# Column sums of the adjacency matrix moved from the first phase to the sweep of the next layer, and row sums by pairwise additions

## The reference

```
# layer 0
adj_hat = adj + eye(n);  d = 1 / sqrt(adj_hat.sum(axis=1))       # row sums
x = x + (d[:,None] * adj_hat * d[None,:]) @ h @ W.T + b
# layer 1: same normalisation, relu
x = x + relu((d[:,None] * adj_hat * d[None,:]) @ (h @ weight))
# layer 2 (attention): uses, besides learned attention matrices,
Rf = S / clip(S.sum(axis=1), 1e-12)                              # row sums again
Rb = S / clip(S.sum(axis=0), 1e-12)[:,None]                      # column sums, S = adj + eye(n)
# layer 3
x = x + (1-t) * (h @ weight) + t * (adj @ (h @ weight))
```

## Time and profile before

| | us |
|---|---|
| median of 3 runs (lowest to highest) | 3489.06 (3486.54 to 3490.57) |
| time of the profiled execution | 3488.64 |
| span of its records | 3486.8 |
| mean granted TensorE clock, share of 2.4 GHz | 0.957 |
| busy in the span: PE, PEld, DVE, ACT, POOL | 3144.3, 2272.6, 2454.0, 1599.1, 2146.4 |

### The profile page before, as it was taken

One profiled execution on the slowest core, in us unless ns is written; L12 is line 12 of the kernel. 1 busy time (PEld: TensorE's weight loads), 2 busy tenths in 40 slices (PEclk: granted clock), 3 DMA queues, 4 the chain that ended last, 5 costly groups with the idle time before them and its releaser, 6 DMA issues. The chain is left out here.

```text
span 3486.8 us, 42119 instructions
## 1 busy us (share of the span) xinstructions
PE 3144.3 (90%) x13212; PEld 2272.6 (65%) x13212; DVE 2454.0 (70%) x3451; ACT 1599.1 (46%) x2357; POOL 2146.4 (62%) x4214
## 2 busy tenths in 40 slices
PE   4999989998699999999976698988899999996899
PEld 3788878885477777777754254544566566664788
DVE  6983410002998889888884799999978999998000
ACT  2211321225566666666653455555555655552200
POOL 1212421124788888888880677877988788886211
PEclk9999999998899999999988899999999999998899
DMA  6643444443122122112211111211222222223254
GB/s 246 223 162 132 130 147 163 163 142 86 44 58 58 58 58 66 54 59 63 65 33 62 47 52 52 62 44 56 57 81 76 73 84 82 74 83 102 91 201 172
DMA packets 140702, 327.59 MB, mean 94 GB/s; under 512 B 15456, under 2 KB 93664, under 8 KB 129248
## 3 DMA queue, kind: packets, MB, share of 16 engines
q1 hardware_dynamic: 140512, 325.30, 29.3%
HBM read 286.70 MB, written 38.54 MB: 93 GB/s over the span
## 5 line engine op out<-in xcount | busy, mean ns | idle before, releaser
L1027 ACT ACTIVATE junk<-E,negp 128x3327 uint8<-128x3327 f32 x208 | 637.3, 3064 | 142.4 <-issue 107.8
L1399 DVE SCALAR_TENSOR_TENSOR U<-E,trial 128x3327 f32<-128x3327 f32 x182 | 678.5, 3728 | 0.0
L922 PE MATMUL bank<-big,adj 128*128 128x512 f32 x1352 | 609.9, 602 | 8.7 <-ACT t L1053 8.7
L922 PEld LDWEIGHTS bank<-big,adj 128*128 128x128 f32 x1352 | 252.9, 192 | 329.2 <-issue 328.1
L294 PE MATMUL bank<-big,E 128*128 128x256 f32 x1664 | 366.2, 381 | 2.4 <-PEq L58 1.7
L882 PE MATMUL bank<-Hc,PT 128*128 128x256 f32 x1248 | 305.1, 396 | 69.2 <-ACT PT L1066 69.2
L294 PEld LDWEIGHTS bank<-big,E 128*128 128x128 f32 x1664 | 315.9, 191 | 49.3 <-issue 6.6
L882 PE MATMUL bank<-Hc,adj 128*128 128x256 f32 x1456 | 335.4, 382 | 10.7 <-ACT adj L1066 10.7
L1361 DVE TENSOR_REDUCE nmax<-E 128x1 f32<-128x3327 f32 x52 | 188.0, 3615 | 207.4 <-ACT E L1070 207.4
L882 PEld LDWEIGHTS bank<-Hc,PT 128*128 128x128 f32 x1248 | 245.9, 199 | 129.9 <-ACT PT L1066 79.7
L882 PEld LDWEIGHTS bank<-Hc,adj 128*128 128x128 f32 x1456 | 277.8, 191 | 72.9 <-issue 23.0
(11 more groups left out here) (248 smaller groups left out, 5937.2 us busy)
## 6 DMA issues: line engine op xcount, KB each, us to landing
adj<-adjT SPq DMA_DIRECT2D x131, 448.0 KB, 3.4
E<-adjT SPq DMA_DIRECT2D x32, 1664.0 KB, 6.9
adj<-adjT SPq DMA_DIRECT2D x104, 384.0 KB, 3.4
adj<-adjT SPq DMA_DIRECT2D x20, 1664.0 KB, 7.0
E<-adjT SPq DMA_DIRECT2D x26, 1216.0 KB, 5.7
xt<-xin SPq DMA_DIRECT2D x52, 128.0 KB, 5.7
x_d<-xn SPq DMA_DIRECT2D x52, 128.0 KB, 1.7
xt<-x_d SPq DMA_DIRECT2D x52, 128.0 KB, 5.2
```

The costliest lines, as they stand in the source:

```text
L922: last = mm(agg[:, 0:w], adj[:, SPAN * (k % 2) + j - AGG[k]], rhs[:, j], start=(j == 0), stop=False)
L1027: go(junk[:, 0:N], E[:, t % DEPTH, 0:N], func, bias=negp[:, t % 2, j:j + 1], scale=1.0, accum_out=acc_[:, t % 2, j:j + 1]).then_inc(summed ...
L1399: V_.scalar_tensor_tensor(out=U[:, 0:N], in0=e, scalar=point, in1=e, op0=ALU.is_ge, op1=ALU.mult, accum_out=found))
```

## The change

Column sums leave front. `layer` with `attention` takes them: after its other work for tile u VectorE reduces all 26 blocks of the buffer and adds them to `cs`; SyncE waits for that as well before it loads the buffer again; the clip and the reciprocal follow at the end of layer 1. In front SyncE waits for the row reduction in place of `columns`.

The row reduction of a tile is no longer one strided reduction to 128 x 128. The 26 blocks are added as 13 pairs into half of the unused buffer `E[:, 3]`, then 6 pairs, then 3 pairs, all contiguous; blocks 0, 1, 2 and 12 are left, and TensorE multiplies each with the column of ones, adding them up in PSUM.

```diff
@@ layer(), sync
                                 sp.wait_ge(agg_done, u - 1)
+                                if attention:
+                                    sp.wait_ge(col_done, u - 1)
                                 sp.dma_start(bufs[par][:, j0:NT], adjT[u][:, j0:NT]).then_inc(adj_in[par], 16)
@@ layer(), vector
+                            if live[0] and attention:
+                                if u >= 2:
+                                    dve.wait_ge(adj_in[par], 8 * u + (0 if par == 0 else -8))
+                                nc.vector.reduce_sum(cpart[:, par], bufs[par][:], axis=AX_X).then_inc(col_part, 1)
+                                dve.wait_ge(col_part, u + 1)
+                                if u >= 1:
+                                    dve.wait_ge(col_done, u)
+                                nc.vector.tensor_tensor(cs[:], cs[:], cpart[:, par], ALU.add).then_inc(col_done, 1)
...
+                            dve.wait_ge(col_done, NT)
+                            nc.vector.tensor_scalar(cs[:], cs[:], CLIP, None, ALU.max).then_inc(col_part, 1)
+                            dve.wait_ge(col_part, NT + 1)
+                            nc.vector.reciprocal(ic[:], cs[:]).then_inc(col_part, 1)
+                            dve.wait_ge(col_part, NT + 2)
@@ front
-            part = xn[:, :, 0:P]
+            folded = E[:, RING - 1].rearrange("p (h j q) -> p h j q", h=2, q=P)
@@ front, sync
                             sp.wait_ge(agg_done, t)
-                            sp.wait_ge(col_done, t)
+                            sp.wait_ge(reduced, t)
                         load_adj(t + 3)
@@ front, tensor
-                            mm(rsum[:, 0:2], part[:, u % 2], ones[:], start=True, stop=True).then_inc(rs_done, 1)
+                            for j in (0, 1, 2, HALF - 1):
+                                last = mm(rsum[:, 0:2], folded[:, u % 2, j], ones[:], start=(j == 0), stop=(j == HALF - 1))
+                            last.then_inc(rs_done, 1)
@@ front, vector
-                        V_.reduce_sum(part[:, u % 2], ring[u % RING].rearrange("p j q -> p q j"), axis=AX_X).then_inc(reduced, 1)
-
-                    def columns(n):
-                        ...
+                        whole, half = ring[u % RING], folded[:, u % 2]
+                        V_.tensor_tensor(half[:, 0:HALF], whole[:, 0:HALF], whole[:, HALF:NT], ALU.add).then_inc(fold, 1)
+                        dve.wait_ge(fold, 2 * u + 1)
+                        V_.tensor_tensor(half[:, 0:6], half[:, 0:6], half[:, 6:12], ALU.add).then_inc(fold, 1)
+                        dve.wait_ge(fold, 2 * u + 2)
+                        V_.tensor_tensor(half[:, 0:3], half[:, 0:3], half[:, 3:6], ALU.add).then_inc(reduced, 1)
...
-                            columns(t)
...
-                        if u < NT - 1:
-                            columns(NT + u)
-                    dve.wait_ge(col_done, sweeps)
-                    V_.tensor_scalar(cs[:], cs[:], CLIP, None, ALU.max).then_inc(fin, 1)
-                    dve.wait_ge(fin, 7)
-                    V_.reciprocal(ic[:], cs[:]).then_inc(fin, 1)
-                    dve.wait_ge(fin, 8)
```

More of the change, by code:

```diff
@@ L246, in layer @@
                 agg_done, agg_copied = s("agg_done"), s("agg_copied")
+                col_part, col_done = s("col_part"), s("col_done")
                 pre, xnew, kept_share = s("pre_added"), s("x_new"), s("kept_share")
@@ L406, in build @@
             agg_done, agg_copied, lifted = s("agg_done"), s("agg_copied"), s("lifted")
-            col_part, col_done, fin = s("col_part"), s("col_done"), s("fin")
+            fin, fold = s("fin"), s("fold")
             pre, xnew = s("pre_added"), s("x_new")
@@ L442, in _ @@
                             sp.wait_ge(agg_done, NT + u)
-                            sp.wait_ge(col_done, NT + u)
                             load_adj(n)
@@ L451, in _ @@
                         sp.wait_ge(agg_done, sweeps)
-                        sp.wait_ge(col_done, sweeps)
                         sp.dma_start(ring[k], adjT[k]).then_inc(first_in, 16)
```

## The result

| | before | after |
|---|---|---|
| median of 11 runs each, us | 3488.46 (3486.54 to 3490.57) | 3497.36 (3493.23 to 3500.20) |
| ratio to before | | 1.0025, interval 1.0016 to 1.0034 |
| profiled execution, its span, us | 3488.64, 3486.8 | 3497.93, 3496.1 |
| mean granted TensorE clock | 0.957 | 0.956 |

A forecast was written before the change was run, and what follows sets the result against it. VectorE was taken to bound sweep 1's early rounds, TensorE its later ones and sweep 2. Sweep 1 -8.5, end of front -0.4, layer 1 +0.6: -8.3 us on 3488.64, forecast about 3481, range 3475 to 3488.

The forecast's parts named there:

- Sweep 1 after the change: Prediction's section on front's first sweep: early rounds follow a chain, later ones TensorE; ends at 261.7, 8.5 us less.
- the chain of 5.1 us: Early rounds of sweep 1: row sum, GpSimd power, layer norm, transposes, products, next row sum in series, 5.1 us a round.
- the first row sum: Start of sweep 1: three more products at the lower clock add 1.3 us, so it comes at 34.9 us.
- The products are dear: Rival, chance 0.05: four row-sum products cost 0.44 us each, rounds grow by 0.9 us more, 16 us in all: 3497.
- binds nowhere: Sweep 1: VectorE's share of a round falls to 4.0 us, so VectorE limits no round.
- the additions' lengths: Sweep 1, VectorE: adding 1664, 768 and 384 elements takes 1.89, 0.96 and 0.56 us, with hand-overs 3.5 instead of 5.84.
- 0.66 us a round for three products: TensorE in sweep 1: three more row-sum products at 0.22 us each, in each of the 26 rounds.
- the lower clock early on: Sweep 1, rounds 0 to 6: TensorE's lower clock raises 5.1 us a round to 5.5 on the mean, 38.6 in all.
- sweep 2 and the end of front: Taking the column sums away gains nothing in sweep 2; without clip and reciprocal front ends 0.4 us sooner.
- Layer 1: Loads go out about 2.1 us later but stay hidden with 0.8 us to spare; 12.33 us a tile; sum +0.6 us.
- The 0.6 us forecast for the first tile's load: Layer 1: load issued at 480.7, landed at 487.6 to 488.6, wanted at 487.52; costs 0.6 us, once.

The follow-up runs named there:

- the fastest kernel: Changed kernel with one strided row reduction again, TensorE summing up to six blocks of tiles 0 to 10 directly, before the transposes: 3474.10 us, ratio 0.9954.

## Why the prediction was wrong

- **The step that failed** stands under "Sweep 1 after the change": "The additions (3.5) lie beside the layer norm (3.64), which hides them", and the chain of 5.1 us built on it. I took two engines side by side as free of each other. They are not, if VectorE reads two SBUF inputs: the chain's power and layer norm became 2.0 us longer, the round 7.03. Against the forecast that is 13.0 us in rounds 0 to 6 (51.6 for 38.6) and 3.6 in rounds 7 to 10 (28.2 for 24.6); with 0.4 more at the first row sum and 0.4 less later it is 16.6 of the 16.7 us by which sweep 1 missed 261.7. The reductions in place of the additions show that no other term of the chain was too small: 4.95 us, 260.1.
- The Trainium skill has the rule (SBUF — State Buffer, Who interferes with whom): a VectorE instruction with two SBUF inputs contends with a GpSimd instruction that reads SBUF, and on this chip a reduction never contends. By the same page of the Trainium skill (SBUF: two separate sides) whichever of the two starts first has the shared ports for its whole length. The traces agree: the power takes 2.08 us beside additions, 1.31 beside a shorter one, 0.55 beside reductions. In sweep 1 every addition kept its length (1.88 to 1.89 us for the first); that VectorE is held in its turn shows only in the attention block (4.22 us for 3.68).
- None of my rivals had the hold, and the rows to price it stood in the trace before: GpSimd's instruction ends when VectorE's does. The first addition takes 1.89 us, so the power could not end sooner. With the 2.0 us measured, the chain is 5.1 + 2.0 = 7.1 a round.
- **None of the rivals names the cause.** "The products are dear" gave 3497 by another route; the products cost 0.66 a round, as priced, and not 0.9 more. That its time agrees with the measured one is chance.
- **A second omission**, which the result doesn't show: the products stand in series between the row reduction and the row sum. The chain had them, but I took it that VectorE "binds nowhere"; had the reduction kept its length, they would have cost 0.65 us in each early round as well.
- **Terms that held**: the additions' lengths; 0.66 us a round for three products (t = 24: 12.77, forecast 12.8); the lower clock early on (rounds 0, 2 and 4 lie 0.94, 0.33 and 0.96 above 7.03, all seven 2.4; 2.8 forecast), though the mean of 0.87 that it leaned on counts a stretch without a clock record as 1.00 (last section); sweep 2 and the end of front 0.7 us better (0.4 forecast); the first row sum 1.7 later (1.3).
- **Layer 1** went by the forecast: the load went out at 760.17 where TensorE wanted the tile at 767.82, and landed within 6.5 to 7.2 us, so with about 0.7 us to spare (0.8 forecast), and the period stayed at 12.33 us. The 0.6 us forecast for the first tile's load did not show: from the second tile's first product to the third's it took 11.45 us (485.06 to 496.51), before 11.44 (476.19 to 487.63). What layer 1 lost instead, 1.4 us in its first tile, came with the clock at 0.50 there; no term of the forecast had it.

## What to carry to other kernels

Before work is put beside work of another engine, ask what the two share. A VectorE operation with two SBUF inputs (an addition of long rows, here) is not free cover for GpSimd: a GpSimd operation of 0.2 us then takes as long as the rest of the addition, and what looks like a busy GpSimd is a waiting one; so give such additions short pieces (5 us better here, still no gain), or do the work by a one-input reduction, which here costs more of VectorE's time and less of the kernel's. Look in the trace that you have for a place where the two kinds of work already stand side by side: this one had it, in another phase. And if an operation is sped up that was the limit, cost the next chain with everything in series in it, the products between the reduction and its reader included. Kernels with one part of the change each showed that one half was worth -11 us, and the other +9 by itself and +20 on top of the first.

## What the runs showed of the hardware

- The hold isn't a share of bandwidth: the addition keeps its length (1.89 us, as much as the one-input reduction of 1664 elements in its place), and the GpSimd operation ends soon after the addition, 0.41 us for the power that takes 0.55 by itself, 0.04 us for the operation of 0.19 (89.91 against 89.87). A VectorE instruction that writes 3336 elements but reads one long row holds nothing (0.19 us beside it), and the hold can fall on VectorE too (4.22 us for a median of 3.68).
- A float32 reduction over blocks 512 bytes apart costs 5.84 us for 3328 elements, 1.6 times the contiguous one (3.61). It also writes 128 sums and not 26; no run separates the two.
- Small weight loads took twice their time early on (1.83 us for 8 at 33.36, 0.97 for 8 at 240.72; 2.90 for 12 at 44.76 in the fastest kernel), although windows from 34 to 38 us and from 44 to 48 us show a granted clock of 1.00. That is no measured clock: the first clock record of a trace lies at 46.7 us in the kernel after, 49.6 with the reductions and 53.3 in the fastest kernel, and what is ahead of it is shown as 1.00. With the reductions the eight loads take 1.83 us at 44.92 and 0.97 at 50.74, so by their lengths TensorE ran at the lower of its two levels, 1.2 GHz, until about the first record.
